# Second layer's attention: values, projections and spare GpSimd work on other beats, and the shifts' transposition ahead of a double values piece

## The reference, cut to what matters

```python
h = _layernorm(x) * (1 + ca) + sa
qkv = h @ W_qkv + b_qkv                       # 16 heads of 8 channels
alibi = minimum(idx[None, :] - idx[:, None], 0)
scores = q k^T * scale + slopes * alibi       # 512 x 512 for each head
w = softmax(scores, axis=-1)
x = x + ga * ((w @ v) @ W_proj + b_proj)
```

## Time and profile before

| what | value |
|---|---|
| median of 3 runs | 1020.94 us (1018.03 to 1024.14) |
| profiled execution | 1019.54 us, span 1017.8 us |
| TensorE matmuls (PE) | 916.2 us busy, 90% |
| VectorE (DVE) | 777.4 us, 76% |
| ScalarE (ACT) | 753.3 us, 74% |
| GpSimd (POOL) | 542.7 us, 53% |
| exponentials, L873 | 832 of 596 ns |
| row maxima, L945 | 242 of 1216 ns |
| values, L767 | 2816 records of 371 ns with VP, 1024 of 332 ns with VD |
| diagonal products, L1047 | 128 of 1273 ns |

### The profile page before, as it was taken

One profiled execution on the slowest core, in us unless ns is written; L12 is line 12 of the kernel. 1 busy time (PEld: TensorE's weight loads), 2 busy tenths in 40 slices (PEclk: granted clock), 3 DMA queues, 4 the chain that ended last, 5 costly groups with the idle time before them and its releaser, 6 DMA issues. The chain is left out here.

```text
span 1017.8 us, 23002 instructions
## 1 busy us (share of the span) xinstructions
PE 916.2 (90%) x8664; PEld 512.1 (50%) x8664; DVE 777.4 (76%) x1319; ACT 753.3 (74%) x1380; POOL 542.7 (53%) x755
## 2 busy tenths in 40 slices
PE   4789988889888999999999889999999999989896
PEld 2233343333436888888888633333333333333564
DVE  4778878888864777767778678989898898994476
ACT  2488878878786566666665379989998898989663
POOL 4376766677633022322210167787877778767343
PEclk8699999999999999999999999999999999999999
DMA  7324432221104622435133020211202031100011
GB/s 185 99 71 122 114 102 76 81 77 51 51 26 116 178 75 83 108 91 156 54 110 88 32 84 6 84 33 57 70 20 75 15 87 33 57 14 15 26 30 52
DMA packets 63598, 73.91 MB, mean 73 GB/s; under 512 B 14136, under 2 KB 46008, under 8 KB 63104
## 3 DMA queue, kind: packets, MB, share of 16 engines
q1 hardware_dynamic: 62336, 69.23, 23.9%
q10 hardware_dynamic: 1152, 3.21, 1.0%
HBM read 39.24 MB, written 2.77 MB: 41 GB/s over the span
## 5 line engine op out<-in xcount | busy, mean ns | idle before, releaser
L873 ACT ACTIVATE at_E<-at_Sb 128x512 f32<-128x512 f32 x832 | 445.1, 596 | 62.2 <-PE at_Sb L719 54.5
L945 DVE TENSOR_REDUCE mx<-at_Mb 128x2 f32<-128x1024 f32 x242 | 281.9, 1216 | 38.1 <-PE at_Mb L682 36.7
L767 PE MATMUL at_Ob<-at_E,VP 128*32 128x256 f32 (+2 forms) x2816 | 204.3, 371 | 2.6 <-POOL at_E L1047 2.0
L1047 POOL TENSOR_TENSOR at_E<-at_E,factor 128x512 f32<-128x512 f32 x128 | 162.3, 1273 | 66.3 <-ACT at_E L873 55.4
L719 PE MATMUL at_Sb<-QP,KP 64*128 64x512 bf16 (+3 forms) x1024 | 188.4, 341 | 9.9 <-ACT full_k L419 3.5
L948 DVE TENSOR_REDUCE mx<-at_Mb 128x2 f32<-128x768 f32 (+1 forms) x128 | 136.7, 1085 | 51.5 <-PE at_Mb L682 50.4
L682 PE MATMUL at_Mb<-KP,QP 62*128 62x512 bf16 x996 | 167.9, 349 | 4.9 <-DVE mx L945 3.5
L1058 POOL TENSOR_SCALAR_AFFINE_SELECT at_E<-at_E 128x512 f32<-128x512 f32 x128 | 80.3, 648 | 70.2 <-ACT at_E L873 70.2
L719 PEld LDWEIGHTS at_Sb<-QP,KP 64*128 64x128 bf16 x1024 | 75.2, 95 | 59.3 <-ACT at_E L873 24.6
L1435 ACT ACTIVATE ex_th<-ex_z 128x512 f32<-128x512 f32 x88 | 55.6, 631 | 63.5 <-DVE ex_z L1488 62.0
L1498 DVE TENSOR_TENSOR ex_hh<-ex_R,ex_th 128x512 f32<-128x512 f32 x88 | 64.5, 733 | 49.5 <-ACT ex_th L1435 48.7
(11 more groups left out here) (213 smaller groups left out, 1464.5 us busy)
## 6 DMA issues: line engine op xcount, KB each, us to landing
QP<-q SPq DMA_DIRECT2D x96, 128.0 KB, 2.4
KP<-k SPq DMA_DIRECT2D x91, 128.0 KB, 2.4
ex_R<-rw_dram SPq DMA_DIRECT2D x32, 256.0 KB, 3.6
ctxN<-Oev SPq DMA_DIRECT2D x16, 256.0 KB, 2.4
denB<-rdram SPq DMA_DIRECT2D x64, 64.0 KB
ex_R<-rw_dram SPq DMA_DIRECT2D x16, 224.0 KB, 4.2
ex_R<-rw_dram SPq DMA_DIRECT2D x16, 192.0 KB, 3.5
ex_R<-rw_dram SPq DMA_DIRECT2D x16, 160.0 KB, 2.9
```

The lines of the kernel that those rows point to most:

```text
L767: last = pe.matmul(Ob[VW * i:VW * (i + 1), 0, q0:q1], weights_of(b, G, kt, i, q0), moving, start=(kt == 0 and q0 == 0), stop=False, skip_g ...
L873: nc.scalar.activation(dst, src, ACT.Exp).then_inc(s["s_read"], 1)
L945: v.tensor_reduce(mx[:, G % 2, :, t % 2, t // 2], src, AX.X, ALU.max).then_inc(s["m_read"], 1)
L1047: p.tensor_tensor(blocks, blocks, factor[:, GROUP * g:GROUP * (g + 1), :], ALU.mult)\
```

## The change

All of it holds for the second layer only; for the first, every condition comes out as before.

- The pieces of values, and with them the copy of `Oev`, come one beat sooner (5 to 11 in place of 6 to 12). So do the transposition of the normalised x (26), the projections of queries (28), keys (4) and values (12) and the output projection (20). The splits and scaled values on GpSimd stay on their beats (the offset from the projection is 2 in place of 1).
- The transposition of the shifts moves from beat 4 of a group to beat 5, where the double values piece now is, and stands ahead of it. ScalarE's copy of the shifts moves to beat 5 too.
- GpSimd's powers and normalisation move from beats 23 and 24 to 19 and 20, the gated weights and bias row from beat 25 to 27.

```diff
--- before.py
+++ after.py
@@ -552,21 +552,21 @@
         SHIFT = 0.0 if causal else ALIBI_SHIFT
 
         LN_AT, Q_AT, K_AT, V_AT, RECIP_AT, CTX_AT, OUT_AT = (
-            (14, 17, 20, 6, 9, 17, 19) if causal else (27, 29, 5, 13, 10, 20, 21))
+            (14, 17, 20, 6, 9, 17, 19) if causal else (26, 28, 4, 12, 10, 20, 20))
         K_LEAD = 2 if causal else 1
-        WEIGHTS_AT = 21 if causal else 25
+        WEIGHTS_AT = 21 if causal else 27
 
         CHUNKS = ({5: ((0, 0, 256),), 6: ((0, 256, 512),), 7: ((1, 128, 512),), 8: ((3, 384, 512), (2, 256, 512))}
                   if causal else
-                  {6: ((0, 0, 256), (0, 256, 512)), 7: ((1, 0, 256),), 8: ((1, 256, 512),), 9: ((2, 0, 256),),
-                   10: ((2, 256, 512),), 11: ((3, 0, 256),), 12: ((3, 256, 512),)})
+                  {5: ((0, 0, 256), (0, 256, 512)), 6: ((1, 0, 256),), 7: ((1, 256, 512),), 8: ((2, 0, 256),),
+                   9: ((2, 256, 512),), 10: ((3, 0, 256),), 11: ((3, 256, 512),)})
         NCH = sum(len(c) for c in CHUNKS.values())
         OEV_AT = max(CHUNKS)
         END = BEATS + OEV_AT - BPG + 1
 
         NEXT_FILLS = {(6, 16): "eln", (6, 20): "elog", (7, 10): "erw"} if causal else {(6, 20): "sln"}
 
-        EARLY = {0: "ln", 2: "q", 5: "k"} if causal else {0: "ln", 2: "q", 5: "k"}
+        EARLY = {0: "ln", 2: "q", 5: "k"} if causal else {0: "ln", 2: "q", 4: "k"}
         FIRST = 2
 
         UNITS = 3 if causal else 4
@@ -582,11 +582,13 @@
                 return [("exp", G, t, t - 4)]
             return [("exp", G, t, 0), ("exp", G, t, 1)]
 
+        TOP = 4 if causal else 3
+
         def fills(beat):
 
             out = []
-            if (beat + 4) % BPG == 0 and 0 <= (beat + 4) // BPG < ALLG:
-                out.append(("max", (beat + 4) // BPG))
+            if (beat + TOP) % BPG == 0 and 0 <= (beat + TOP) // BPG < ALLG:
+                out.append(("max", (beat + TOP) // BPG))
             n, at = divmod(beat, BPB)
             if beat in EARLY:
                 out.append((EARLY[beat], 1))
@@ -806,22 +808,18 @@
                 for _, G, t, c in slots_S(beat):
                     key_score(G, t, c)
                 tops = [name for name in fills(beat) if name[0] == "max"]
-                if causal:
-                    for name in tops:
-                        max_T(name[1])
+                for name in tops:
+                    max_T(name[1])
                 for G, off in zip(*chunks(beat)):
                     values(G, off)
                 for name in fills(beat):
-                    if name[0] == "max":
-                        if not causal:
-                            max_T(name[1])
-                    elif name[0] == "ln":
+                    if name[0] == "ln":
                         norm_T(name[1])
                     elif name[0][0] == "e":
                         start_experts(name[0])
                     elif name[0] == "sln":
                         start_spikes()
-                    else:
+                    elif name[0] != "max":
                         project(*name)
                 if not causal and out_of(beat) is not None:
                     out_proj(out_of(beat))
@@ -1077,13 +1075,13 @@
                     p.tensor_tensor(xb, xb, sb["ctxT"][:], ALU.add).then_inc(ex["xup"], 1)
                 if EARLY.get(beat) in ("q", "k"):
                     split(EARLY[beat], 1)
-                if at == LN_AT - 4 and 2 <= n + 2 <= last_b:
+                if at == (LN_AT - 4 if causal else 19) and 2 <= n + 2 <= last_b:
                     front_powers(p, sb, s, n + 2)
-                if at == LN_AT - 3 and 2 <= n + 2 <= last_b:
+                if at == (LN_AT - 3 if causal else 20) and 2 <= n + 2 <= last_b:
                     normalise(n + 2)
-                if at == Q_AT + (2 if causal else 1) and FIRST <= n + 2 <= last_b:
+                if at == Q_AT + 2 and FIRST <= n + 2 <= last_b:
                     split("q", n + 2)
-                if not causal and at == K_AT + 1 and FIRST <= n + 1 <= last_b:
+                if not causal and at == K_AT + 2 and FIRST <= n + 1 <= last_b:
                     split("k", n + 1)
                 if causal and at == 3 and FIRST <= n + 1 <= last_b:
                     split("k", n + 1)
@@ -1096,7 +1094,7 @@
                 if causal and (n, at) == (6, 18):
                     p.wait_ge(s["s_read"], s_slot[("eln", 0)] + 1)
                     expert_split(p, sb, ex, 0, sb["h_hi0"][:], sb["h_lo0"][:])
-                if not causal and at == V_AT + 1 and 1 <= n + 1 <= last_b:
+                if not causal and at == V_AT + 2 and 1 <= n + 1 <= last_b:
                     decayed(n + 1)
                 if not causal and at == CTX_AT - 2 and 1 <= n <= last_b:
                     finish_context(p, sb, s, n - 1)
```

## The result

The changed kernel takes 1032.81 us (median of 4 runs, 1031.72 to 1036.49), the kernel before, on the same chip, 1021.02: ratio 1.0123, interval 1.0095 to 1.0151. It is slower, by 11.8 us where 7 were forecast. The profiled execution took 1032.48 us, its span 1030.7.

What follows compares the result with a forecast made beforehand. TensorE sets the beat and all engines are nearly full, so the order of work decides. Five full batches +1.2 us each (6.0), first -0.8, seventh +1.7, last 0: +7, so 1028 us, range 1013 to 1037.

Steps and rivals of the forecast that it cites:

- The likeliest case: The prediction's own forecast: second layer's attention slower by 7 us in total, 1028 us; chance 0.45.
- (a): Key group, projection in beat 4: waits 0.13 us for its bank; next max score 2.84 us after beat 3's.
- (c): Shifts' transposition in beat 5, ahead of the double piece: waits for the projection's bank, 1.0 us (values 0.85).
- (d): Beat 8's max score comes 7.76 us after beat 3's, before 7.37: key and value groups each 0.4 slower.
- the ring's wait: Three score banks in rotation: the transposition waits until ScalarE has read the projection's bank, 1.0 us for keys.
- (e): Values piece in beat 10 waits 0.5 us for GpSimd's diagonal product behind the split, twice a batch.
- (f): GpSimd's earlier powers and normalisation: third diagonal product 0.3 us late for beat 24; last group's 1.93 us wait removed.
- (g): Shifts' copy nearly 2 us later: rows covered with 0.25 us to spare, context product's input with about 0.2.
- (h): End of the stage, and the output projection's wait for VectorE one beat sooner: both unchanged, cost 0.
- The first (the ring doesn't bite): Rival: the transposition finds its bank free in key, value and query fills, 19 us less, 1009; chance 0.18.
- The second (no second price): Rival: GpSimd's diagonal products aren't late for the values pieces, 7 us less, 1021; chance 0.22.
- The third: Rival: rows or context late, another 0.3 us in each of 28 groups, 1037; chance 0.15.

## Why the prediction was right, and where it was short

The likeliest case held in sign, and in mechanism for the key, value and last groups; the size was 7 for 11.8 us. That it came so near is in part luck. The third group was forecast at 0 and grew by 0.75 us in the mean of batches 1 to 6, and the last batch, also forecast at 0, by 4.3. Against this the last group gained 0.4 more than forecast, 0.23 of it the slow clock in the kernel before, and the value group cost 0.2 less. The signs named did come: the waits for `full_k`, `VP` and `full_q`, no wait for the shifts, the values pieces' wait behind each split. A full batch took 46.2 to 46.6 us, a little over the 45 to 46 stated. By its steps:

- **(a), (c), (d)** came out to 0.1 us in the key group, and the rest of (d) was confirmed by what is left when the other terms are out: +0.47 and +0.30 against 0.4 and 0.4. But the ring's wait is no term by itself. Taking it out (the transposition behind the double piece) gave the key group nothing. It is shared with the next wait, GpSimd's, and only a group's whole length can be priced.
- **(e)** was right in place and size: 0.5 forecast; the edit that removes it gave 0.52 and 0.41 a batch in six batches, 5.6 us in all against the prediction's 0.5 x 11 = 5.5 (there are twelve such places).
- **(f)** was right in direction. The third product's 0.3 didn't come (beats 24 and 25 take 1.11); by the prediction's own figures, 8.6 less 8.4, it was 0.2. The last group gained 1.0 for 0.6. The weights cost nothing. The moves alone give 9 to 11.5, and within the change 1.1 by the medians: the sum had this, since it set the ring's 1.0 against the 1.93.
- **(g)** The rows' cover was as thin as said: 9 waits, the longest 0.7. The context product missed its input by 0.21 in batch 2 where 0.2 was to spare.
- **(h) is the step that failed**: "The output projection's wait for VectorE stays as it is, one beat sooner: 0". I moved the output projection forward and the context product back, and priced that product only for what is behind it on GpSimd, not for who reads it. Its reader stands idle 1.42 us in batch 2, and 2.89 in the last batch, with slow matmuls behind, where the kernel before had 0.54 to spare in batch 2. Nor did the wait for VectorE stay as it was: in the kernel before TensorE's matmuls show none of their own for it, and with the context product early 0.52 is left. Putting the projection back was worth 1.4 to 4.2 us, and 4.2 by the medians on top of the later splits (1027.2 to 1023.04), of the 4.8 between the forecast 1028 and 1032.81; it removes the wait in the full batches but not in the last. With the product early, beat 20 was 0.69 shorter in six batches and 4.1 in the last, some 8 us, my estimate of what the late product costs; the other beats took it back, and some of the 0.69 may only have moved to beat 18. In the last batch the late producer is the cause: the spread of the reciprocals is issued 21.0 us after the batch's first exponential, where it was 19.9, and takes 5.6 to `ctxT`'s start, where it took 5.2; the reader came a beat sooner on top, and there (h) had 0. The terms by batch: first -0.8 forecast and +0.07 measured, full ones +6.0 and +7.24, seventh +1.7 and +1.46, last 0 and +4.3.
- **The rivals.** The first (the ring doesn't bite) fell by its own point of decision: ScalarE's `full_k` releases the transposition 1.0 after TensorE is there. The second (no second price) fell with the later splits. The third had the place, a late context product, but the wrong victim: it charged 0.3 in every group, and the cost is in the third group and the last batch. Its rule of a fixed cost counted from the second issue isn't needed for the result: the rows' waits are mostly tenths. The range ended at 1013, so it left out the first rival's own 1009 and not only its lower half.

What stays open: the first batch, whose gain of 0.8 didn't come. The granted clock was at 0.50 for 6.8 us near its start in the change and for 3.4 in the kernel before; what that cost was not taken apart. Nor was why the last batch varies so much between versions (39.2 to 43.2). The time from the spread's issue to `ctxT` was 5.5 to 6.7 us in them, and a fall of the clock lengthens what is late. Executions of one kernel differ in this too: over the 50 of the kernel before on the four chips of the experiments, the mean granted clock ran from 0.971 to 0.985 and the time from 1026.26 down to 1016.85. With the splits later and the projection back the third group is still 0.5 longer than before: the max score waits for VectorE there, and why VectorE is late was not tested. I didn't try an earlier context product that avoids both the rows' queue and VectorE's statistics.

## What to carry to other kernels

When a step is moved forward, list what it reads as well as what it holds up: each producer's end against the new start, those that the same change delays above all. Two waits behind one another share their cost, so test a change's parts one at a time in both directions, alone and taken out; here a third of the change alone was a gain of 9 to 11.5 us that the rest hid. In a queue with one order, such as SP's, every DMA that is put forward is a delay for the ones it passes (beat 15 behind the earlier spread).

## What the runs showed of the hardware

- **TensorE's clock fell after short pauses.** In the second layer's attention, over all the traces here, nine waits of TensorE were longer than 2 us, from 2.07 (late rows) to 2.98 (splits later, last batch). In each case the granted clock then read 0.50, the 1.2 GHz level, for 3.4 to 6.8 us, and in full batches a max score took 0.61 where it takes 0.39. Shorter waits did so now and then: one of the six of 1.93 us in the kernel before, one of 1.83 with the transposition behind the double piece, and in the last batch two in a row, of 0.59 and 1.15 with the projection on beat 21 and of 0.44 and 0.43 with the values alone sooner. The waits of 1.25 to 1.62 in the full batches of the change had no such tail. So a long wait on TensorE was dearer than its length, and removing the 1.93 us waits, as GpSimd's moves do, also removed an occasion for it.
- **VectorE's small scaling waited for GpSimd.** 128x4 elements took 1.2 us beside a GpSimd product of two tensors in five of six batches, and 0.17 elsewhere, while the maxima (TENSOR_REDUCE) ran beside GpSimd unchanged. The Trainium skill, SBUF — State Buffer, section Who interferes with whom, says that VectorE in its two-port mode, which a tensor_scalar can enter, and GpSimd exclude each other for a whole instruction, and that a reduction never contends. The trace agrees on both counts (1198 ns at the median against 171; maxima 1218 ns in both kernels).
- **A releaser that isn't one.** The list of waits put the output projection's wait down to VectorE's maxima, in batches where `ctxT` ended 0.1 before the start. In the kernel with the context product early the same name was right: `ctxT` had ended 3.5 us before, and 0.52 of wait was left. The prediction had taken that name for the cause.
